# Self attention of a decoder: scores as row tiles, values as column tiles on turned probabilities, and x loaded with the weights

## Reference

```python
q = (_layernorm(x, qn_g, qn_b) @ Wq + bq).reshape(B, C, H, hd).transpose(0, 2, 1, 3)
kv = (_layernorm(x, kvn_g, kvn_b) @ Wkv + bkv).reshape(B, C, 2, H, hd)
...
q = q * scale
k = k * scale
q = _rotary(q, x)
k = _rotary(k, x)
qn = _layernorm(q, ln_g, ln_b)
kn = _layernorm(k, ln_g, ln_b)
scores = jnp.einsum('bhqd,bhkd->bhqk', qn, kn) / jnp.sqrt(jnp.asarray(hd, x.dtype))
causal = jnp.tril(jnp.ones((C, C), bool))
scores = jnp.where(causal, scores, jnp.finfo(scores.dtype).min)
w = jax.nn.softmax(scores, axis=-1)
a = jnp.einsum('bhqk,bhkd->bhqd', w, v)
out = a.transpose(0, 2, 1, 3).reshape(B, C, Dm) @ Wo + bo
```

## Time and profile before

| | |
|---|---|
| median of 3 runs | 1935.43 us (1934.2 to 1939.39) |
| time of the profiled execution | 1936.83 us |
| its span | 1935.0 us |
| mean granted TensorE clock | 0.929 |
| TensorE (PE) busy | 1633.1 us, 84% of the span |
| VectorE (DVE) busy | 1414.9 us, 73% |
| GpSimd (POOL) busy | 1149.5 us, 59% |
| ScalarE (ACT) busy | 777.1 us, 40% |
| end of the first block's work | 241.1 us |

### The profile page before, as it was taken

How to read it: one execution, slowest core, us unless ns; L and a number is a source line. 1 busy time by engine, 2 the same in 40 slices (tenths; PEclk the granted TensorE clock), 3 DMA queues, 4 the chain that set the end, 5 groups by cost and what they waited for, 6 DMA issues and landing times. The chain is left out here.

```text
span 1935.0 us, 25602 instructions
## 1 busy us (share of the span) xinstructions
PE 1633.1 (84%) x8098; PEld 942.0 (49%) x8098; DVE 1414.9 (73%) x2776; ACT 777.1 (40%) x1847; POOL 1149.5 (59%) x979
## 2 busy tenths in 40 slices
PE   3579969574527799999999999989999999999887
PEld 2457846352213355545545555545545555554444
DVE  7956345766786878878888888787887787786455
ACT  1344345451343353433444434444444344343242
POOL 4234246003025677976877887767897777776542
PEclk9789889687767999999999999999999999999979
DMA  2000071100040000000000000000000000000020
GB/s 59 1 1 1 1 255 35 44 1 28 0 151 33 1 1 1 1 35 1 1 1 1 1 35 1 1 1 1 1 1 1 1 1 1 1 1 1 1 66 22
DMA packets 27804, 38.20 MB, mean 20 GB/s; under 512 B 4628, under 2 KB 24344, under 8 KB 27416
## 3 DMA queue, kind: packets, MB, share of 16 engines
q1 hardware_dynamic: 27672, 36.57, 5.6%
HBM read 35.51 MB, written 1.05 MB: 19 GB/s over the span
## 5 line engine op out<-in xcount | busy, mean ns | idle before, releaser
L1865 POOL TENSOR_TENSOR stream_acc<-stream_acc,stream_p 128x512 f32<-128x512 f32 x448 | 570.8, 1277 | 212.4 <-ACT stream_p L1788 208.1
L1788 ACT ACTIVATE stream_p<-stream_lowered 128x512 f32<-128x512 f32 (+1 forms) x480 | 302.4, 630 | 678.3 <-DVE stream_lowered L1925 676.9
L1730 PE MATMUL stream_banks<-stream_p,stream_v 128*128 128x512 f32 (+1 forms) x960 | 490.0, 592 | 0.9 <-ACT stream_p L1788 0.9
L1925 DVE TENSOR_TENSOR stream_lowered<-stream_banks,stream_shift_all 128x512 f32<-128x512 f32 (+1 forms) x480 | 329.8, 687 | 187.5 <-PE stream_banks L1717 161.2
L1932 DVE TENSOR_REDUCE stream_tops<-stream_banks 128x1 f32<-128x512 f32 (+1 forms) x512 | 322.6, 630 | 35.2 <-PE stream_banks L1703 35.2
L1703 PE MATMUL stream_banks<-stream_k_t_hi,stream_q_t_hi 128*128 128x512 bf16 (+1 forms) x512 | 185.8, 363 | 33.5 <-DVE stream_tops L1932 31.7
L1730 PEld LDWEIGHTS stream_banks<-stream_p,stream_v 128*128 128x128 f32 (+1 forms) x960 | 175.2, 190 | 57.5 <-ACT stream_p L1788 2.7
L1717 PE MATMUL stream_banks<-stream_q_t_hi,stream_k_t_hi 128*128 128x512 bf16 (+1 forms) x480 | 182.8, 381 | 0.0
L1717 PE MATMUL stream_banks<-stream_q_t_hi,stream_k_t_lo 128*128 128x512 bf16 (+1 forms) x480 | 181.9, 379 | 0.0
L1717 PE MATMUL stream_banks<-stream_q_t_lo,stream_k_t_hi 128*128 128x512 bf16 (+1 forms) x480 | 181.9, 379 | 0.0
L1870 POOL TENSOR_TENSOR stream_by_cos<-stream_by_cos,stream_by_sin 128x512 f32<-128x512 f32 x96 | 120.3, 1253 | 50.6 <-DVE stream_by_sin L1960 50.4
(11 more groups left out here) (401 smaller groups left out, 3102.8 us busy)
## 6 DMA issues: line engine op xcount, KB each, us to landing
memory_raw_t<-in_ctx_t SPq DMA_DIRECT2D x4, 1601.0 KB, 8.9
cross_ctx_t<-in_ctx_t SPq DMA_DIRECT2D x4, 1601.0 KB, 7.5
memory_raw<-in_ctx SPq DMA_DIRECT2D x4, 1536.0 KB
cross_w_raw_q<-in_L_xattn_Wq SPq DMA_DIRECT2D x1, 2048.0 KB, 11.9
cross_w_raw_o<-in_L_xattn_Wo SPq DMA_DIRECT2D x1, 2048.0 KB, 19.4
moe_raw_up<-in_L_ffn_wi SPq DMA_DIRECT2D x8, 256.0 KB, 4.8
model_x<-in_x SPq DMA_DIRECT2D x1, 1024.0 KB, 5.4
ffn_raw_fc<-in_L_ffn_w_fc SPq DMA_DIRECT2D x1, 1024.0 KB, 5.0
```

Source lines behind the costliest of these rows:

```text
L1730: nc.tensor.matmul(ps[:, 2 + n, :], v[0:r, g % 2, t, :], p32[0:r, step % 4, :], start=(t == 0), stop=(t == KT - 1)).then_inc(weighed, 1)
L1788: nc.scalar.activation(p32[0:r, step % 4, :], lowered[0:r, step % 3, :], ACT.Exp, scale=SCALE).then_inc(p32_ready, 1)
L1865: nc.gpsimd.tensor_tensor(acc[0:r, g % 2, cols], acc[0:r, g % 2, cols], p32[0:r, step % 4, :], ALU.add).then_inc(acc_ready, 1)
L1925: nc.vector.tensor_tensor(lowered[0:r, step % 3, :], ps[0:r, step % 2, :], shift_all[0:r, g % 2, n * HALF:(n + 1) * HALF], ALU.add).then_i ...
```

## The change

Start. x and the identity are loaded inside `self_attention`, and the 14 loads that the projections need are issued behind them with no wait between; the mask and the output bias follow under a semaphore of their own, and `w_o` in four loads into padded rows after GpSimd has cleared it. `k_own` is gone. GpSimd clears `w_o` (1024 columns) and `v` (4096 columns, since a head of `v` now has 32). The factor of the double norm comes from one square root in place of two, and the row's length from a second chain, `size`.

```diff
+                sp.dma_start(x[:], w["x"].rearrange("b (t p) d -> p (b t) d", p=P)).then_inc(x_loaded, 16)
+                sp.dma_start(ident[:], w["ident"]).then_inc(x_loaded, 16)
...
+                sp.dma_start(causal[:], w["causal"]).then_inc(late_loaded, 16)
+                sp.dma_start(b_o[:], w["bo"].partition_broadcast(P)).then_inc(late_loaded, 16)
+                sp.wait_ge(zeroed, 1)
+                for j in range(4):
+                    sp.dma_start(w_o[PAD * j:PAD * j + HD0], w["Wo"].rearrange("(g j d) n -> j d g n", j=4, d=HD0)[j]).then_inc(out_loaded, 16)
...
-                nc.gpsimd.memset(v[:, :, :, HD0:HD0 + 1], 1.0)
-                nc.gpsimd.memset(k_own[:], 0.0).then_inc(zeroed, 1)
-
-                gp.wait_ge(xn_ready, TILES)
-                gp.wait_ge(loaded, 16 * 17)
-                nc.gpsimd.tensor_tensor(x[:], x[:], bcast(b_o[:], 1, TILES), ALU.add).then_inc(bias_added, 1)
+                nc.gpsimd.memset(w_o[:], 0.0).then_inc(zeroed, 1)
+                nc.gpsimd.memset(v[:], 0.0).then_inc(zeroed, 1)
+                gp.wait_ge(loaded, 16 * 14)
...
+                nc.vector.tensor_scalar(rs[:, 0, :], mean_var[:, :, 1], 1.0 + 1e-5, 1e-5 * 1e-5, ALU.mult, ALU.add).then_inc(rs_ready, 1)
+                link(nc.vector.tensor_scalar(size[:, 0, :], mean_var[:, :, 1], 1e-5, None, ALU.add))
+                link(nc.vector.reciprocal(size[:, 0, :], size[:, 0, :]))
+                link(nc.vector.tensor_tensor(size[:, 1, :], size[:, 0, :], mean_var[:, :, 1], ALU.mult))
+                nc.vector.tensor_scalar(size[:, 1, :], size[:, 1, :], float(DM) * float(HD0) ** -0.5, None, ALU.mult).then_inc(size_ready, 1)
                 ve.wait_ge(rs_done, 1)
...
+                link(nc.vector.reciprocal(rs[:, 2, :], rs[:, 1, :]))
```

```diff
+                ve.wait_ge(zeroed, 2)
                 take_qkv(0)
                 for t in range(TILES):
+                    waves_of(t)
+                    if t >= 1:
+                        invert(t - 1)
+                    rotate(t)
                     if t + 1 < TILES:
                         take_qkv(t + 1)
...
+                    vary(t)
+                invert(TILES - 1)
```

```diff
+                def score(u):
+                    b, g = divmod(u, GROUPS)
+                    if u >= 1:
+                        pe.wait_ge(mx_ready, QT * u)
+                    for t in range(QT):
+                        for i in range(4):
+                            rows = slice(PAD * i, PAD * (i + 1))
+                            last = nc.tensor.matmul(ps[:, 4 + i, t * P:t * P + (t + 1) * P], q_t[rows, g, b * SEQ + t * P:b * SEQ + (t + 1) * P],
+                                                    k_t[rows, g, b * SEQ:b * SEQ + (t + 1) * P], start=True, stop=True)
                     last.then_inc(scores_ready, 1)
...
+                def weigh(u):
+                    b, g = divmod(u, GROUPS)
+                    pe.wait_ge(pt_ready, u + 1)
+                    if u >= 1:
+                        pe.wait_ge(att_ready, u)
+                    if b >= 1 and g == 0:
+                        pe.wait_ge(out_taken, b)
+                    for s in range(2):
+                        for c in range(QT):
+                            for i in range(4):
+                                moving = p_t[:, u % 2, i * SEQ:(i + 1) * SEQ] if c == 0 else p_t[:, u % 2, 4 * SEQ + i * P:4 * SEQ + (i + 1) * P]
+                                weight = v[:, QT * b + c, 4 * g + i, :] if s == 0 else ones[:]
+                                last = nc.tensor.matmul(ps[PAD * i:PAD * (i + 1), 3, s * SEQ + c * P:(s + 1) * SEQ], weight, moving,
+                                                        start=(c == 0), stop=(c == QT - 1))
                     last.then_inc(pv_done, 1)
...
+                def project_out(b):
+                    pe.wait_ge(att_ready, GROUPS * (b + 1))
...
+                for u in range(UNITS_SELF + 2):
+                    if u + 2 < UNITS_SELF:
+                        score(u + 2)
+                    if u < UNITS_SELF:
+                        turn_probs(u)
+                    if u >= 2 and (u - 2) % GROUPS == GROUPS - 1:
+                        project_out((u - 2) // GROUPS)
+                    if 1 <= u <= UNITS_SELF:
+                        weigh(u - 1)
...
+                def mask(u):
+                    ve.wait_ge(scores_ready, u + 1)
+                    if u >= 3:
+                        ve.wait_ge(probs_t, u - 2)
+                    for t in range(QT):
+                        span = slice(t * P, t * P + (t + 1) * P)
+                        for i in range(4):
+                            last = nc.vector.tensor_tensor_reduce(sm[:, u % 3, i, span], ps[:, 4 + i, span], causal[:, SEQ - (t + 1) * P:SEQ],
+                                                                  1.0, 3.0 * MASKED, ALU.add, ALU.max, mx[:, u % 4, t, i:i + 1])
+                        last.then_inc(mx_ready, 1)
+
+                def normalise(u):
+                    b, g = divmod(u, GROUPS)
+                    ve.wait_ge(pv_done, u + 1)
+                    link(nc.vector.reciprocal(inv[:], ps[:, 3, SEQ:2 * SEQ]))
+                    nc.vector.tensor_tensor(att[:, g, b * SEQ:(b + 1) * SEQ], ps[:, 3, 0:SEQ], inv[:], ALU.mult).then_inc(att_ready, 1)
...
+                for k in range(UNITS_SELF + GROUPS):
+                    if k < UNITS_SELF:
+                        mask(k)
+                    if k >= 2 * GROUPS - 1 and k % GROUPS == GROUPS - 1:
+                        add_out(k // GROUPS - 1)
+                    if 0 <= k - 3 < UNITS_SELF:
+                        normalise(k - 3)
```

More of the change, by code:

```diff
@@ L303, in _ @@
-                ac.wait_ge(loaded, 16 * 17)
+                ac.wait_ge(rs_ready, 1)
+                nc.scalar.activation(rs[:, 1, :], rs[:, 0, :], ACT.Sqrt).then_inc(rs_done, 1)
+                ac.wait_ge(size_ready, 1)
+                nc.scalar.activation(size[:, 2, :], size[:, 1, :], ACT.Sqrt).then_inc(size_done, 1)
+                ac.wait_ge(size_done, 1)
+                ac.wait_ge(loaded, 16 * 14)
                 for b in range(BATCH):
+                    for t in range(QT * b, QT * (b + 1)):
+                        last = nc.scalar.activation(turn[:, t], wave[:, :, t % QT, :], ACT.Identity, scale=size[:, 2, t:t + 1])
+                        last.then_inc(turn_ready, 1)
@@ L388, in _ @@
                 pe.wait_ge(qkt_ready, TILES)
-                def score(j):
-                    t, g, nk = j // GROUPS, j % GROUPS, keys(j)
-                    if j >= 2:
-                        pe.wait_ge(scores_taken, j - 1)
-                    for half_group in range(2):
-                        keep = slice(2 * half_group, 2 * half_group + 2)
-                        last = nc.tensor.matmul(
-                            ps[:, 4 + 2 * (j % 2) + half_group, :].rearrange("p (h n) -> p h n", h=2)[:, :, 0:nk],
-                            q_t[:, g, t * P:(t + 1) * P],
-                            k_own[:, g, keep, t // QT * SEQ:t // QT * SEQ + nk], start=True, stop=True)
-                    last.then_inc(scores_ready, 1)
@@ L414, in weigh @@
-                def weigh(j):
-                    t, g, n = j // GROUPS, j % GROUPS, keys(j) // P
-                    pe.wait_ge(pt_ready, j + 1)
-                    if g == 0 and t >= 2:
-                        pe.wait_ge(att_ready, t - 1)
-                    for i in range(4):
-                        h = 4 * g + i
-                        for c in range(n):
-                            last = nc.tensor.matmul(ps[:, 2 + t % 2, h * (HD0 + 1):(h + 1) * (HD0 + 1)], p_t[:, j % 2, i * n + c, :],
-                                                    v[:, t // QT * QT + c, h, :],
-                                                    start=(c == 0), stop=(c == n - 1))
-                    last.then_inc(pv_done, 1)
@@ new lines, in turn_probs @@
+                def turn_probs(u):
+                    pe.wait_ge(probs_ready, u + 1)
+                    if u >= 1:
+                        pe.wait_ge(pt_ready, u)
+                    for i in range(4):
+                        for t in range(QT):
+                            for c in range(t + 1):
+                                to = i * SEQ + t * P if c == 0 else 4 * SEQ + i * P
+                                last = nc.tensor.transpose(ps[:, to // 512, to % 512:to % 512 + P],
+                                                           sm[:, u % 3, i, (t + c) * P:(t + c + 1) * P], ident[:])
+                    last.then_inc(probs_t, 1)
@@ new lines, in project_out @@
+                def project_out(b):
+                    pe.wait_ge(att_ready, GROUPS * (b + 1))
+                    if b == 0:
+                        pe.wait_ge(out_loaded, 16 * 4)
+                    for q in range(QT):
+                        for g in range(GROUPS):
+                            last = nc.tensor.matmul(ps[:, 3, q * DM:(q + 1) * DM], att[:, g, (QT * b + q) * P:(QT * b + q + 1) * P], w_o[:, g, :],
```

(2 more changed lines are left out.)

287 lines of the change are left out of this document (113 added, 174 removed).

## The result

The changed kernel takes **1875.7 us** (median of 4 runs, 1874.1 to 1877.9) against 1936.5 (4 runs, 1934.2 to 1939.4) beside it: ratio 0.969, 95% interval 0.967 to 0.970. Forecast were 1918 us and a range from 1894. The direction was right; the gain is 61 us where 17 were forecast.

The account below looks back on a forecast made before the run. VectorE was taken to bound the rotation, TensorE the attention. First scores 29.6 us earlier and an attention 12 us longer (141 against 128.7) gave 17.3 us less: 1935.4 - 17.3 = 1918 us, range 1894 to 1968.

Parts of the forecast that it names:

- Start and rotation: Work before the first scores: first rotation 14.6 us earlier, seven tile intervals 11.7 us less, last tile 3.3 us less.
- Values and sums: Attention, TensorE: 16 products, 32 records a unit; 5.2 us one by one, 1.3 to 1.6 with four column tiles, 2.7 taken.
- A product overlaps with its neighbour by one record: Values and sums on TensorE: issue order limits overlap to one record, so the time halves to 2.7 us a unit.
- Scores: Attention, TensorE: 8 products, 16 records a unit; 2.7 us without overlap, 1.9 taken, with weight loads one by one.
- Switches: Attention, TensorE: three changes a unit between row tiles, whole array and column tiles, 0.1 us each.
- Mask: Attention, VectorE: eight mask-and-maximum operations a unit, 2.9 us, as much as before the change.
- the reciprocal: Attention, VectorE: reciprocal of 256 columns instead of 16 sums, 1.8 us a unit.
- the unit: Attention step of four heads and both query tiles, 16 in all: TensorE 6.5 us, VectorE 5.2 us.
- projections, filling, waits and clock: Attention besides its units: projections 14, filling 7, three waits of 1, a last chain 5, half clock 8 us.
- all four tiles overlap: Rival, attention: TensorE needs 5.3 us a unit or less, VectorE bounds at 5.2 plus waits; 1898 us, chance 0.20.
- The clock did not fall: Rival, attention: waits between a unit's phases keep TensorE's clock at 0.72, 8.9 us a unit; 1961 us, chance 0.10.
- half clock again: Both ends of the attention: 8 us added for TensorE at half clock, as in the kernel before.

## Why the prediction was wrong

- **Start and rotation: right.** `xn` at 11.12 (11.1 forecast), `by_cos` at 19.97 (21.0), 6.83 us a tile (7.0; one operation a tile is held by GpSimd, 1.29 for 0.42 us), first scores at 79.5 (82.8). 33.0 us gained, 29.6 forecast. They are more than half of the 60; only the clearing was tested by a run, the rotation's part rests on these rows.
- **Values and sums: the step that failed.** "A product overlaps with its neighbour by one record", 2.7 us; the profile has 1.5. The bounds were 1.3 and 5.2, and I chose half of the upper one by an argument on the order of issue for which no row stood: a product's second record was to hold up the next product's first. The windows show four products' records starting together. By the factor of 2.38 for three column tiles in the Trainium skill, "TensorE: Matmul & The Clock Gate", part 3, an estimate for the values is 5.2 / 2.38 = 2.2 us; the trace has less.
- **Scores: too high, by the same kind of step.** 1.9 us, because sixteen weight loads would go one by one; they take 0.94 with the loads. The Trainium skill's 3.07 for four row tiles ("TensorE: Matmul & The Clock Gate", part 3) stands beside 3.1 measured (2.88 by 0.94), here with two records a product.
- **Switches: about as forecast.** I took 0.3 us a unit for three. Twelve transposes step by 1.46 us (102.32 to 103.78), where eight stepped by 0.87 in the kernel before, so twelve would have taken 1.31: 0.15 more. The sums step by 0.79 ahead of scores (117.78 to 118.57), the values by 0.65 ahead of sums in the same mode: 0.14 more. The drain between tiling modes that the Trainium skill describes ("TensorEngine Tiling", section "Tiling Modes") may be in these, but the rows do not part it from the next phase's first weight load.
- **Mask: 2.9 forecast, 2.23 measured.** I added up lengths where the step counts. With the reciprocal right (1.8; 1.76), VectorE needs 4.48 us a unit, not 5.2; my own terms, 2.9 + 1.8 + 0.4, add up to 5.1.
- **So the unit.** TensorE 6.5 forecast, 3.8 measured; the unit is VectorE's 4.48, and 16 x 2.0 = 32 of the 39 us by which the attention was overestimated (141 against 101.7) come from there. Of these, 21 are TensorE's, from 6.5 down to the 5.2 forecast for VectorE, and 11 are VectorE's, from 5.2 to 4.48. The other 7 were projections, filling, waits and clock: 37 forecast, 101.7 - 71.7 = 30 left over. That is a remainder, not a reading, since not every unit took 4.48: the first steps from scores to scores took 4.1 to 4.6.
- **The rival "all four tiles overlap"** was the right one, with 0.20, and still put VectorE at 5.2 us; so its time of 1898 and the range's lower end missed as well. Its ground, that each tile has its own bank, holds for the scores only: the four heads' values share bank 3, on partitions of their own, and overlapped all the same. The clock did not fall: it was 0.97 from 90 to 160 us and 1.00 from 160 to 182, where the kernel before had 0.65 at its end and the forecast had counted half clock again.

## What to carry to other kernels

When one engine's cost hangs on an unmeasured overlap, the forecast's range must reach to the bound that the other engine sets, and that bound is worked out with steps between back-to-back instructions, not with their lengths. Products in different tiles are to be issued side by side: order alone was worth 26 of 61 us. When a bound moves to another engine, its longest single operation is next, and moving it pays only as far as the new engine's order lets its result come in time.

## What the runs showed of the hardware

- Column tiles run ahead of the order of issue by about one product: in the order head by head, the next tile's values and this tile's sums start within 0.01 us of one another (107.67 and 107.68).
- Two f32 records a product do not hinder the overlap of tiles: four records of four heads lay in a window of 0.1 us, and four more in each of the next two, and 32 records took 1.5 us.
- A table load on ScalarE took 1.28 us. Logarithm and exponential in turns brought one for nearly each; with a set that holds both, loaded once, none came between them.
- GpSimd's clearing held a VectorE operation with one large input (`xn`, 5.79 for 2.67 us), not only those with two.
